# Shorter lags between scores, transposes and value products in a causal attention and mixture kernel

## What is computed

```python
xn = layernorm(x)
q, k, v = (einsum('bse,hde->bhsd', xn, W) + b for each of the three)
att = softmax(where(causal, -inf, q @ k.T / sqrt(64))) / sqrt(64)
attention = (att @ v).reshape(b, s, h * dh) @ proj      # a plain reshape of (b, h, s, d)
base = xn @ W.T
gate = softmax(l2norm(xn @ Wp.T + bp) @ l2norm(sim) * exp(min(temp, CLAMP_MAX)))
experts = sum over e of (gate[e] if e is the largest else 0) * (xn @ Wd[e].T) @ Wu[e].T
out = x + attention + base + experts
```

## Time and profile before

| what | value |
|---|---|
| median of 3 runs | 1348.05 us (1347.9 to 1348.14) |
| the profiled execution, its own time | 1347.42 us |
| its span, first to last instruction | 1345.7 us |
| busy: PE, PEld | 1330.3 us (99%), 1131.7 us (84%) |
| busy: DVE, ACT, POOL | 1106.3 us (82%), 1085.9 us (81%), 997.7 us (74%) |
| granted PE clock | 1.00 (2.4 GHz) |

### The profile page before, as it was taken

The page is one execution under the profiler, slowest core; times in us unless marked ns, Lnnn a source line. Parts: engine busy times, 40 slices in busy tenths (PEclk is TensorE's granted clock), DMA queues, the critical chain, the costliest instruction groups (busy, mean ns, idle before and its releaser), DMA issues.

```text
span 1345.7 us, 34453 instructions
## 1 busy us (share of the span) xinstructions
PE 1330.3 (99%) x10783; PEld 1131.7 (84%) x10783; DVE 1106.3 (82%) x4001; ACT 1085.9 (81%) x3162; POOL 997.7 (74%) x1443
## 2 busy tenths in 40 slices
PE   7999999999999999999999999999999999999998
PEld 5788888888888888888888888888888888888887
DVE  8978888788787878878788787888878888788785
ACT  6887887888788887887888788788888887888785
POOL 7887777778777777777777768777677876778664
PEclk9999999999999999999999999999999999999999
DMA  6455444544544445454444544454454454545541
GB/s 155 95 119 118 103 112 113 122 104 111 125 107 116 105 113 123 103 122 110 116 103 115 123 103 115 112 122 110 103 124 113 103 122 112 122 95 119 118 103 48
DMA packets 112561, 150.59 MB, mean 112 GB/s; under 512 B 18239, under 2 KB 47230, under 8 KB 112382
## 3 DMA queue, kind: packets, MB, share of 16 engines
q1 hardware_dynamic: 111086, 147.97, 46.8%
q10 hardware_dynamic: 1296, 0.42, 0.2%
HBM read 10.69 MB, written 4.19 MB: 11 GB/s over the span
## 4 chain that ended last, share of the span: by engine, by line
PE 95%; ACT 1%; SPq 0%; POOL 0%; DVE 0%; DMA 0%; issue 0%; DVEq 0%; POOLq 0%
PE zp L1323 22%; PE ptp L1297 20%; PE jobp L1167 13%; PE scores L1285 9%; PE scores L1288 7%; PE outp L1335 7%; PE jobp L1172 6%; PE scores L1266 4%; PE scores L1263 3%; PE jobp L1182 1%; PE outp L1344 1%; PE jobp L1187 1%; PE jobp L1360 0%; PE jobp L1177 0%; ACT prob L721 0%; PE outp L1349 0%
## 5 line engine op out<-in xcount | busy, mean ns | idle before, releaser
L632 POOL TENSOR_TENSOR prob<-prob,rden 128x128 f32<-128x128 f32 (+3 forms) x1024 | 712.4, 720 | 247.2 <-DVE rden L971 240.7
L982 DVE CUSTOM_DVE_ANT_0 prob<-scores,mask 128x128 f32<-128x128 f32 (+3 forms) x1024 | 471.7, 488 | 199.8 <-issue 133.3
L721 ACT ACTIVATE prob<-prob,nmax 128x128 f32<-128x128 f32 (+3 forms) x1024 | 567.5, 559 | 12.1 <-DVE nmax L982 5.4
L1297 PE MATMUL ptp<-ident,prob 128*128 128x128 f32 x2560 | 366.9, 274 | 2.1 <-ACT pt L732 1.5
L1297 PEld LDWEIGHTS ptp<-ident,prob 128*128 128x128 f32 x2560 | 295.0, 140 | 27.4 <-POOL prob L632 5.0
L1323 PE MATMUL zp<-pt,v_sb 128*64 128x64 f32 (+3 forms) x4096 | 307.7, 303 | 0.0
L732 ACT ACTIVATE pt<-ptp 128x128 f32<-128x128 f32 (+3 forms) x512 | 221.2, 432 | 102.8 <-PE ptp L1297 102.8
L1323 PEld LDWEIGHTS zp<-pt,v_sb 128*64 128x64 f32 x4096 | 221.6, 137 | 51.2 <-issue 19.7
L994 DVE COPY pt<-ptp 128x128 f32<-128x128 f32 (+3 forms) x512 | 243.3, 475 | 3.9 <-PE ptp L1297 3.1
L571 POOL CAST k_low<-k_lo 64x512 fp32r<-64x512 f32 x256 | 156.0, 609 | 78.0 <-DVE k_lo L866 68.1
L1285 PE MATMUL scores<-k_twice,q_parts 128*128 128x384 f32 (+1 forms) x512 | 200.9, 392 | 0.0
(11 more groups left out here) (192 smaller groups left out, 2003.3 us busy)
## 6 DMA issues: line engine op xcount, KB each, us to landing
k_twice<-k_hi SPq DMA_DIRECT2D x506, 128.0 KB, 2.3
q_parts<-q_lo SPq DMA_DIRECT2D x256, 128.0 KB, 2.4
q_parts<-q_hi SPq DMA_DIRECT2D x254, 128.0 KB, 2.3
xin<-in_L_attn_x_dram SPq DMA_DIRECT2D x16, 256.0 KB, 3.1
xres<-in_L_attn_x_dram SPq DMA_DIRECT2D x16, 256.0 KB, 3.1
out_dram<-osb SPq DMA_DIRECT2D x15, 256.0 KB, 2.6
pt<-in_L_attn_Wq_dram SPq DMA_DIRECT2D x1, 512.0 KB, 4.8
pt<-in_L_attn_Wk_dram SPq DMA_DIRECT2D x1, 512.0 KB, 5.6
```

The source lines that it names most:

```text
L632: nc.gpsimd.tensor_tensor(part, part, scale, ALU.mult).then_inc(pn_ready, 1)
L721: nc.scalar.activation(part, part, ACT.Exp, bias=nmax[:, s % NROT, h:h + 1], scale=-1.0, accum_out=den[:, s % NROT, h:h + 1]).then_inc(p_r ...
L982: nc.vector.tensor_tensor_reduce(out=prob[:, s % NROT, h, 0:cols], in0=scores[bank][:, first_col:first_col + cols], in1=mask[:, S - cols:S ...
L1297: done = nc.tensor.transpose(ptp[h][:, P * j:P * j + P], prob[:, s % NROT, h, P * j:P * j + P], ident[:])
```

## The change

The transposes follow the scores by two steps, and a pair's value products its first scores by six (its last transposes by one step). The value products now stand in third steps directly behind the scores, ahead of the transposes; the projection quarters move to second steps (one, at step 19, stays in a fourth), ahead of the transposes there. The v job of step 22 goes to step 5, ahead of that step's transposes. DVE makes the low part of the keys in third steps, ahead of the reciprocals, and other low parts in other steps (`subtracted`). POOL pads the low keys behind the scaling of the second step, that is ahead of the third step's scaling; the router's products (L651, L652) follow the padding in step 2, and the router's root (L642, L645) in step 6. Several `STEP_...` constants move by one to four steps. In third steps ACT does its exponentials ahead of its copy.

```diff
-LAG_T = 3
-LAG_PV = (9, 9)
-LAG_Z, LAG_LOW_Z = 10, 11
-LAG_OUT = ((27, 31, 35, 39), (25, 27, 31, 35))
+LAG_T = 2
+LAG_PV = 6
+LAG_Z, LAG_LOW_Z = 7, 7
+LAG_OUT = ((25, 29, 33, 37), (25, 29, 33, 35))
...
-V_STEPS = (29, 30, 2, 6, 10, 14, 18, 22)
+V_STEPS = (29, 30, 2, 5, 6, 10, 14, 18)
...
-STEP_EVAC, STEP_BASE, STEP_OUT, STEP_FINAL, STEP_LORA = 20, 24, 21, 21, 24
-STEPS_STATS, STEP_AGGR, STEP_VAR = (5, 9), 17, 17
-STEP_RSTD, STEP_CENTRE, STEP_SCALE = 18, 19, 21
+STEP_EVAC, STEP_BASE, STEP_OUT, STEP_FINAL, STEP_LORA = 20, 24, 21, 22, 24
+STEPS_STATS, STEP_AGGR, STEP_VAR = (2, 6), 18, 18
+STEP_RSTD, STEP_CENTRE, STEP_SCALE = 19, 20, 22
...
-STEP_PRODUCTS, STEP_UNORM, STEP_EXPERTS = 3, 4, 7
+STEP_PRODUCTS, STEP_UNORM, STEP_EXPERTS = 2, 6, 10
...
-STEP_SUMS, STEP_LOGITS, STEP_WEIGHTS, STEP_FIRST, STEP_PARTS = 5, 6, 9, 10, 13
+STEP_SUMS, STEP_LOGITS, STEP_WEIGHTS, STEP_FIRST, STEP_PARTS = 6, 9, 10, 14, 14
...
+def subtracted(s):
+    if s % NBLK == 2:
+        return [s - 2]
+    return [] if s % NBLK == 3 else [s if s % NBLK == 1 else s - 1]
...
                     normalise(c, s)
-                    if s in JOBS and JOBS[s][0] == "k" and not (last and s in AHEAD):
-                        pad_low_keys(c, s)
+                    if s % NBLK == 1 and not (last and s - 1 in AHEAD):
+                        pad_low_keys(c, s - 1)
...
                 maximum(c, s, 1)
+                products = s % NBLK == 2
+                if products:
+                    jobs(c, s, last)
                 router_early(c, s)
...
                 if not tail:
                     score(c, s, first)
+                if not tail and s == V_STEPS[3]:
+                    job(c, s)
+                if s % NBLK == 1:
+                    quarters(c, s, first, tail)
+                p = due(s, LAG_PV, NBLK, first, tail)
+                if p is not None:
+                    for h in range(2):
+                        values(c, p, h)
                 unit = due(s, LAG_T, 1, first, tail)
                 if unit is not None:
                     transpose(c, unit)
-                if not tail and s in JOBS and not (last and s in AHEAD):
+                if not tail and s in JOBS and s != V_STEPS[3] and not (last and s in AHEAD):
                     job(c, s)
                 if s == STEP_OUT and not first:
                     transpose_sum(c, tail)
-                for h in range(2):
-                    p = due(s, LAG_PV[h], NBLK, first, tail)
-                    if p is not None:
-                        values(c, p, h)
...
+                if s % NBLK != 1:
+                    quarters(c, s, first, tail)
```

More of the change, by code:

```diff
@@ L565, in pad_low_keys @@
                 made = c.fixed(c.job(s))
-                scaled = 0 if setup else c.fixed(c.head(s, 1))
+                scaled = 0 if setup else c.fixed(c.head(s + 1, 1))
                 if not setup:
@@ L781, in step @@
                         nc.scalar.activation(lg[:, 3, :, :], lg[:, 2, :, :], ACT.Exp).then_inc(lg_exp, 1)
+                if s == V_STEPS[3]:
+                    job(c, s)
                 unit = due(s, LAG_T, 1, first, tail)
-                if unit is not None:
+                products = s % NBLK == 2
+                if unit is not None and not products:
                     evacuate_pt(c, unit)
@@ L788, in step @@
                     exponentials(c, s)
+                if unit is not None and products:
+                    evacuate_pt(c, unit)
+                if not tail and s != V_STEPS[3]:
                     if s in evacuated(s) and s in JOBS and not (last and s in AHEAD):
@@ L1073, in router_late, with jobs @@
                         .then_inc(gated_ready, 1)
+            def jobs(c, s, last):
+                for js in subtracted(s):
+                    if js in JOBS and not (last and js in AHEAD):
+                        job(c, js)
             def step(c, s, first=False, last=False, tail=False):
@@ L1099, in step @@
                     job(c, UNITS - 1, back=1)
-                for js in evacuated(s):
-                    if js in JOBS and not (last and js in AHEAD):
-                        job(c, js)
+                if not products:
+                    jobs(c, s, last)
                 for half, due_step in enumerate(FIRST_STATS if first else STEPS_STATS):
@@ L1139, in _ @@
             reciprocals(c, -1)
-            evacuate_pt(c, -3)
             evacuate_pt(c, -2)
-            low_z(c, -2)
             evacuate_pt(c, -1)
@@ L1361, in transpose_sum, with quarters @@
                 done.then_inc(y_ready, 1)
+            def quarters(c, s, first, tail):
+                for o in range(NOCT):
+                    for quarter in range(4):
+                        n = due(s, OCT_STEPS * o + LAG_OUT[o][quarter], UNITS, first, tail)
+                        if n is not None:
+                            project(c, NOCT * n + o, quarter)
             def step(c, s, first=False, last=False, tail=False):
@@ L1376, in step @@
                     transpose_sum(c, tail)
-                for h in range(2):
-                    p = due(s, LAG_PV[h], NBLK, first, tail)
-                    if p is not None:
-                        values(c, p, h)
-                for o in range(NOCT):
-                    for quarter in range(4):
-                        n = due(s, OCT_STEPS * o + LAG_OUT[o][quarter], UNITS, first, tail)
-                        if n is not None:
-                            project(c, NOCT * n + o, quarter)
+                if s % NBLK != 1:
+                    quarters(c, s, first, tail)
                 if tail:
@@ L1426, in project_last @@
                 done.then_inc(o_ready, 1)
-            transpose(c, -3)
+            transpose(c, -2)
             project(c, -2, 2)
-            for h in range(2):
-                values(c, -2, h)
-            transpose(c, -2)
             transpose(c, -1)
```

6 lines of the change are left out of this document (2 added, 4 removed).

## The result

The changed kernel takes 1560.97 us (median of 4 runs, 1559.06 to 1562.49), where the kernel before takes 1348.09 on the same chip: 1.158 times as long, 95% interval 1.1565 to 1.1593, or 213 us more. Forecast were 1473 in a range of 1405 to 1530. The direction and the kind of wait are as forecast, the sum is not: 125 us were forecast.

A forecast was written before the change was run, and what follows sets the result against it. PE, busy 99% without a hole, was taken as the bound. (4.6 + 3.9) us x 15.5 batches = 132, less 6 and 1 is 125; on 1347.4, with 0.6 for the median, 1473 us, range 1405 to 1530.

The forecast's parts named there:

- the ordinary wait: The second head's third transposes on PE wait for POOL's third scaling, 0.56 us in nearly every pair.
- T: The start of a fourth step's scores on PE; times within a pair are counted from it in us.
- Together 3.9 a batch: Added waits of transposes from work ahead of them: 0.8 (step 2), 1.2 (step 6), 1.5 (xt), 0.4 (small operations).
- 4.6: Waits in us a batch from the shorter lag: 7 x 0.56 at third transposes plus 0.70 in step 21.
- Small operations of the router in steps 10 and 14, and the final sum in 22 … I take 0.4: Work ahead of a fourth step's first maximum, taken to add 0.4 us a batch, between 0 and 1.
- Above, 5.5: Upper bound in us a batch on the 3.9 for work not covered by POOL's idle 0.5.
- For xt 1.5 was taken: Step 26: DVE's wait in step 25 for ACT's copies of xt adds 1.5 us a batch, up to 2.1.
- Moves of statistics, v jobs and copies lie beside PE and cost nothing as long as these engines keep their idle fifth: Moved work on the engines beside PE was priced at nothing while those engines stay idle a fifth of the time.
- the gain of 6 and 1: 6 us saved by transposes following value products instead of scores, 1 us by fewer waits at the program's end.
- The fourth transposes wait as well: Rival: fourth transposes also wait, 0.4 us in seven pairs of a batch, giving 1518 us; chance 0.12.
- Faster: Rival: third scaling ends before T + 2.72 in most pairs, so no wait appears: 1341 us; chance 0.04.
- The rule on headroom: Skill page's rule: weight loads at 84% leave 215 us free on TensorE to absorb waits; 1341 us, chance 0.02.

The follow-up runs named there:

- e: The changed kernel with the router's small operations put back where the kernel before had them: 1521.78 us.
- j: The changed kernel with the transposes again three steps behind the scores, value products still ahead of them in third steps: 1429.72 us.
- l: The changed kernel with transposes again three steps behind the scores, and statistics and the router's operations back at their old steps: 1393.97 us.
- c: The kernel before with only the value products one step later, in third steps ahead of the transposes: 1356.12 us.
- f: The changed kernel with the input's statistics back at steps 6 and 10 in place of 2 and 6: 1561.65 us.
- d: The changed kernel with the third step's reciprocals moved ahead of the fourth step's first maximum: 1547.65 us.
- g: The changed kernel with the edits of d, e and f together: 1492.09 us.
- a: The kernel before with only the transposes' lag behind the scores cut from three steps to two: 1543.11 us.
- b: The kernel before with only the moves in VectorE's and GpSimd's order and the step constants; lags and PE's order as before: 1526.34 us.
- h: The changed kernel with GpSimd's low parts of the next inputs put behind the padding of step 25: 1606.74 us.

## Why the prediction was wrong

**Right.** That PE's stream has no hole, so that a late input costs its whole delay. The place and cause of the ordinary wait: third scaling at T + 3.28 for T + 3.23, fourth at T + 5.79 for T + 5.87, no wait of the fourth transposes except in step 21 (0.84 for 0.70) and none in step 20. The padding itself at nothing in an ordinary pair. Of what was to be seen, PE at 91% and `ptp` behind POOL's `prob` are there, also the long waits in steps 4, 8 and 28. But the waits are 338, counted by head, where some 100 were to be seen, and a part of the idle time stands in front of scores, which was named as a sign of being wrong.

**Wrong: the size of the sum.** 88 us lie between 1473 and 1561. By the account, at 16.2 us for each us a batch:

- *"Together 3.9 a batch"* and *"4.6"*. The waits of transposes are 10.6 a batch instead of 8.5, some 34 us. Most of it is the ordinary wait, 0.76 and not 0.56 in seven places (1.4 a batch), since data come 0.06 later, PE is there 0.06 earlier, and starts again in two places, once for each head. Step 8 lacked the clamp and the pauses (0.4). *"Small operations of the router in steps 10 and 14, and the final sum in 22 … I take 0.4"*: the waits there are 1.0 above the ordinary one. Run e shows the router's part of all this at 39 us. (The bound "Above, 5.5" is more than its own terms give, 0.8 + 1.2 + 2.1 + 1.0 = 5.1.) Two terms are right in size by luck. Step 4 (1.37 for 1.36) is a longer ordinary wait and 0.6 for the router's product in place of 0.8. For xt 1.5 was taken, and steps 27 and 28 without their 0.4 of scores are 1.5 over the ordinary wait; but 1.2 of it are waits of the second transposes at step 27, for which nothing was forecast: VectorE's wait for ScalarE is 22.9 / 15 = 1.5, not 0.86, and it holds up the second reciprocals as well. This wait's row in the list of waits:

```profile
DVE xq_lo L867 <- ACT xq_hi L703: 22.9, 15, 1.5
```

- *"Moves of statistics, v jobs and copies lie beside PE and cost nothing as long as these engines keep their idle fifth".* The step that failed worst. The condition held (VectorE 72% busy, ScalarE 73%, GpSimd 64%), and the moves cost all the same. Waits in front of other work than transposes are 1.7 a batch, 28 us: scores wait 1.0 at steps 3, 11 and 15 for maxima that stand behind moved work and 0.4 at step 27 for the padding; the rest is about what the v job moved to step 5 waits for VectorE, 0.3 (799.82 to 800.59, 0.77 for 0.47). The forecast followed a late maximum to the third scaling but not to the next user of its PSUM bank, the first scores; and it asked for padding by T + 2.1, which holds in an ordinary pair (T + 0.9) and not behind VectorE's wait at step 25. Without the new lag the rest of the change costs 82 us (run j), of which 15 are the statistics and 21 the router, and by the trace of run l 13 the v job. The v job's row in the changed kernel's list of waits:

```profile
PEld jobp L1188 <- DVE q_lo L881: 5.3, 15, 0.4
```

- *The clock.* Half clock, 0.88 a batch, 14 us, was not in the sum (last section).
- The rest is the gain of 6 and 1 that doesn't appear in the time, and 6 from counting 15.5 batches where the time goes with 16.2. The single gain is there, as at 876.74 to 876.93, two transposes behind value products; the other parts outweigh it, as in run c.

**The parts do not add.** Lag, moves and value products alone cost 195, 178 and 8 us, together (with the quarters, the moved v job and ScalarE's order) 213; at the old lag all the rest costs 82 and the lag on top of it 131. Forecast were 132 for what the lag makes of both. It agrees with the 131 only by chance, since waits of scores and transposes take each other's place (run f).

**The rivals.** *The fourth transposes wait as well* did not occur in the change, but it does as soon as the third scaling is made earlier (run d): the loop is as tight there as the sum said. *Faster* needed reciprocals ahead of the maximum; d has them and still takes 1548, since steps 4, 8 and 27 and the fourth transposes remain. "It decides at 0.56 us" held for one pair's wait only.

**The rule on headroom.** Weight loads fell from 84% to 73% while the time rose by 213 us. Run l, with 80%, still pays 46 us for its waits. The Trainium skill, page "Perfetto Trace Analysis", section "Identifying the Most-Contended Engine", takes the weight loads' share, together with the matmul rate as a share of the peak, as the better measure of how near TensorE is to its limit; here the measured times differ from that: the share left over is no room that could take up a wait. The same page, section "Optimization Strategy", says to look for the gaps on the engine and for the semaphore behind each; that is what the tables above do, and the trace of before had few such gaps (transposes that wait for GpSimd: 5.0 us in 20 waits).

## What to carry to other kernels

Where one engine runs without a hole, price a shorter lag by following every moved operation to *all* that waits for what stands behind it: the next step's data and also the next user of the same PSUM bank. Waits in such a loop neither add nor come out one by one (d, e and f: 13, 39 and 0 us alone, 69 together in g). A sum that puts small terms "beside" the path at nothing came out too low here; its upper end should allow for all of them at their longest. Undoing one part at the old lag (j) told more than running one part alone (a, b), because a part alone can open a wait that the whole does not have.

## What was not expected of the hardware

PE's granted clock fell to half inside the kernel, ten times: behind the long wait of step 8 in eight of the sixteen batches, and in the first batch at steps 4 and 20. In the kernel before it stays at 1.00 up to its last microseconds. Stretches around one wait of step 8 (columns: us, busy us of PE, PEld, DVE, ACT, POOL with instructions, granted clock, DMA share, GB/s):

```profile
904.00:905.00 1.00, 0.39 (x4) 0.25 (x3) 1.00 (x4) 0.80 (x3) 0.92 (x2) 1.00 0.00 0
905.00:906.00 1.00, 0.00 (x0) 0.00 (x0) 0.56 (x6) 0.89 (x3) 1.00 (x3) 1.00 0.00 0
906.00:907.00 1.00, 0.70 (x4) 0.47 (x5) 0.00 (x0) 0.36 (x1) 1.00 (x3) 0.96 0.00 0
907.00:908.00 1.00, 1.00 (x5) 0.90 (x5) 0.25 (x1) 0.90 (x5) 1.00 (x2) 0.50 0.88 209
908.00:910.00 2.00, 2.00 (x8) 1.71 (x7) 0.99 (x3) 0.69 (x1) 0.78 (x1) 0.50 0.15 35
```

PE waits from 904.4 to 906.1, works again, and then from 907 to 910 is granted 0.50, 1.2 GHz: the work behind the wait pays a second time. Where the long waits are shortened (e, g) three or none of these stretches are left inside the kernel; where a second long one is added at step 27 (h) the mean granted clock is 0.968 and 2.66 us a batch are lost. The Trainium skill, page "TensorE: Matmul & The Clock Gate", section "HAM oscillation — how this bites in real kernels", describes this for waits on DMA between groups of matmuls, after which the work starts at the low clock. The trace agrees that work behind a wait runs at half clock, here for waits on GpSimd, but not that it starts so: from 906.06 to 906.9 PE is granted 1.00 and only then 0.50.
